# Attention of a graph network block: softmax weights normalised ahead of their transposes, and the product with v on four column tiles

## The reference

```python
x = _layernorm(x + _L0_gnn_ref(x, adj, ...))   # two layers: u = h W h' masked by adj, exp, divide, @ h_lin, norm, relu
x = _layernorm(x + _L1_gnn_ref(x, adj, adj, Wq, Wk, Wv, bv, Wo, bo))

# _L1_gnn_ref, 12 heads of 32 features
q, k, v = x @ Wq.T, x @ Wk.T, x @ Wv.T + bv
scores = einsum('bqhd,bkhd->bhqk', q, k) * scale + (adj + adj)[:, None]
row_nonzero = any(scores != 0, axis=-1, keepdims=True)
p = nan_to_num(softmax(where(row_nonzero, scores, -inf)))
out = einsum('bhqk,bkhd->bqhd', p, v).reshape(b, n, h)
return out @ Wo.T + bo
```

## Time and profile before

| | |
|---|---|
| median of three runs | 2868.6 us (2867.44 to 2870.93) |
| profiled execution | 2869.89 us, its span 2868.0 us |
| PE busy | 2794.6 us, 97% |
| PEld busy | 1790.0 us, 62% |
| DVE busy | 2406.5 us, 84% |
| ACT busy | 1770.5 us, 62% |
| POOL busy | 1657.6 us, 58% |
| DMA | 112.21 MB, 39 GB/s in the mean |

### The profile page before, as it was taken

The page is one execution under the profiler, slowest core; times in us unless marked ns, Lnnn a source line. Parts: engine busy times, 40 slices in busy tenths (PEclk is TensorE's granted clock), DMA queues, the critical chain, the costliest instruction groups (busy, mean ns, idle before and its releaser), DMA issues.

```text
span 2868.0 us, 69803 instructions
## 1 busy us (share of the span) xinstructions
PE 2794.6 (97%) x24768; PEld 1790.0 (62%) x24768; DVE 2406.5 (84%) x8042; ACT 1770.5 (62%) x4107; POOL 1657.6 (58%) x2097
## 2 busy tenths in 40 slices
PE   7999999999999999999999999999999999999996
PEld 4566666666665666666666656666666666566664
DVE  5788888888888888888888888888888888888886
ACT  4556666556665556665566655566655666555664
POOL 2556565556565565655565655656555656555554
PEclk9999999999999999999999999999999999999998
DMA  4001011111011010111010110101110101101000
GB/s 151 30 32 45 21 46 40 41 36 34 32 43 43 32 45 21 45 40 44 33 35 31 43 43 31 45 21 45 40 45 32 41 25 43 43 32 45 21 27 21
DMA packets 55976, 112.21 MB, mean 39 GB/s; under 512 B 4944, under 2 KB 37712, under 8 KB 55632
## 3 DMA queue, kind: packets, MB, share of 16 engines
q1 hardware_dynamic: 55632, 107.76, 11.0%
HBM read 82.58 MB, written 25.17 MB: 38 GB/s over the span
## 4 chain that ended last, share of the span: by engine, by line
PE 86%; DVE 10%; ACT 2%; issue 1%; POOL 0%; DMA 0%; DVEq 0%; SPq 0%; POOLq 0%; ACTq 0%
PE psum L1250 62%; PE psum L1260 11%; PE psum L1311 9%; PE psum L1404 3%; PE psum L1378 2%; DVE z L1016 2%; DVE nT_lo L813 2%; DVE pT_lo L811 1%; DVE rs L876 1%; DVE qk_lo L813 1%; ACT qk_hi L536 1%; ACT pT_hi L536 1%; DVE st L915 1%; DVE o L888 1%; DVE y L907 1%
## 5 line engine op out<-in xcount | busy, mean ns | idle before, releaser
L596 ACT ACTIVATE w<-s,nmax 128x128 f32<-128x128 f32 x1536 | 479.4, 403 | 1.9 <-DVE nmax L846 1.9
L1250 PE MATMUL psum<-hT_hi,w_hi 128*128 128x512 f16 x1152 | 439.1, 381 | 13.3 <-POOL hT_lo L379 11.9
L1250 PE MATMUL psum<-hT_lo,w_hi 128*128 128x512 f16 x1152 | 438.7, 381 | 0.0
L1250 PE MATMUL psum<-hT_hi,w_lo 128*128 128x512 f16 x1152 | 438.4, 381 | 0.0
L536 ACT ACTIVATE nT_hi<-psum 128x512 f16<-128x512 f32 x384 | 230.1, 599 | 271.0 <-PE psum L1250 270.9
L463 POOL TENSOR_TENSOR fold<-fold 128x384 f32<-128x384 f32 (+4 forms) x640 | 342.8, 536 | 50.1
L846 DVE CUSTOM_DVE_ANT_0 s<-psum,adj 128x128 f32<-128x128 f32 x1536 | 341.0, 284 | 30.8 <-PE psum L1378 30.0
L463 POOL TENSOR_TENSOR fold<-s 128x768 f32<-128x768 f32 x128 | 242.3, 1893 | 193.5 <-DVE nmax L846 193.5
L387 POOL TENSOR_TENSOR hl_lo<-hl_raw,hl_hi 128x384 fp32r<-128x384 f32 x256 | 245.3, 963 | 147.5 <-ACT hl_hi L536 143.6
L811 DVE TENSOR_TENSOR pT_lo<-psum,pT_hi 128x512 f16<-128x512 f32 x384 | 253.2, 683 | 37.7 <-ACT pT_hi L536 37.5
L536 ACT ACTIVATE pT_hi<-psum 128x512 f16<-128x512 f32 x384 | 222.0, 598 | 85.3 <-PE psum L1260 85.1
(11 more groups left out here) (133 smaller groups left out, 7948.5 us busy)
## 6 DMA issues: line engine op xcount, KB each, us to landing
xTin<-xT SPq DMA_DIRECT2D x32, 768.0 KB, 4.7
xres<-x SPq DMA_DIRECT2D x32, 768.0 KB, 4.6
out<-y SPq DMA_DIRECT2D x128, 192.0 KB, 1.9
adjn<-adj SPq DMA_DIRECT2D x32, 256.0 KB, 4.9
adjT_sb<-adjT SPq DMA_DIRECT2D x32, 256.0 KB, 5.0
adj<-adj SPq DMA_DIRECT2D x32, 256.0 KB, 2.8
x<-weights SPq DMA_DIRECT2D x4, 576.0 KB, 5.4
s<-weights SPq DMA_DIRECT2D x3, 576.0 KB, 6.4
```

Source lines behind the costliest of these rows:

```text
L596: last = nc.scalar.activation(w[:, m], s[b % 2][:, m], ACT.Exp, bias=nmax[b % 2][:, m:m + 1], scale=-1.0)
L1250: last = mm(dst, a, b, start=(i == 0), stop=(i == total - 1))
```

## The change

`v` loses its column of ones, and the row sums come from ACT: the exponentials have an `accum_out` into `sums`. Once all 12 heads of a graph are done, DVE makes reciprocals (`rcp`) and `rs`, and POOL multiplies w by rs in three parts (`norm`), in place, before PE transposes it. w has two buffers. In `pv` the operands change places: 32 columns of v are stationary, 128 columns of pT move, and the four heads j of a step write to the four 32-partition quarters of one bank. The output so comes out transposed, and the split into oT_hi and oT_lo reads it straight from the bank of `pv`; the stage `to` on PE and the product `o` on DVE go. The folds on POOL stop at 16 columns and DVE does the rest in one `tensor_reduce`. `v_raw` has two buffers instead of four. The bank lists and the orders of PE, DVE, ACT and POOL are new; pt(3), norm(3) and rs(3) move to the next pass. The order on SP stays.

```diff
-        w = sb("w", [HEADS, TOK])
+        w = [sb(f"w{i}", [HEADS, TOK]) for i in range(2)]
@@ banks
-                "pt": pt_lo, "pv": o_ok, "to": to_lo, "po": y2_ok}
+                "pt": pt_lo, "pv": to_lo, "po": y2_ok}
...
-        TAIL = (("pv", 3), ("to", 3), ("po", 3), ("fin", 2), ("fin", 3), ("y2_power", 3), ("store", 3))
+        TAIL = (("rs", 3), ("norm", 3), ("pt", 9), ("pt", 10), ("pt", 11), ("pv", 3), ("po", 3), ("fin", 2), ("fin", 3), ("y2_power", 3), ("store", 3))
@@ POOL
-                for n, src_ok, done in ((TOK // 2, None, fold1), (TOK // 4, fold1, fold2), (TOK // 8, fold2, fold3),
-                                        (TOK // 16, fold3, fold4), (TOK // 32, fold4, fold5),
-                                        (TOK // 64, fold5, fold6)):
+                for n, src_ok, done in ((TOK // 2, None, fold1), (TOK // 4, fold1, fold2), (TOK // 8, fold2, fold3)):
...
-                nc.gpsimd.tensor_tensor(total[b % 2][:], fold[:, :, 0], fold[:, :, 1], ALU.add)\
-                    .then_inc(s_tot.sem, 1)
+            def norm(run, b, r):
+                p = run.of("norm", b)
+                if p is None:
+                    return
+                if r == 0:
+                    pool.wait_ge(rs_ok.sem, p.upto(rs_ok, b + 1))
+                part = slice(TILES * r, TILES * (r + 1))
+                nc.gpsimd.tensor_tensor(w[b % 2][:, part], w[b % 2][:, part],
+                                        rs[b % 2][:, part, None].to_broadcast([128, TILES, TOK]), ALU.mult)\
+                    .then_inc(pn_ok.sem, 1)
@@ ACT exps
-                if b > 0:
-                    act.wait_ge(pt_full.sem, p.upto(pt_full, KB * (b - 1) + chunk))
+                if b >= 2:
+                    act.wait_ge(pt_full.sem, p.upto(pt_full, KB * (b - 2) + chunk))
+                    act.wait_ge(rcp_ok.sem, p.upto(rcp_ok, b - 1))
...
-                    last = nc.scalar.activation(w[:, m], s[b % 2][:, m], ACT.Exp, bias=nmax[b % 2][:, m:m + 1],
-                                                scale=-1.0)
+                    last = nc.scalar.activation(w[b % 2][:, m], s[b % 2][:, m], ACT.Exp, bias=nmax[b % 2][:, m:m + 1],
+                                                scale=-1.0, accum_out=sums[b % 2][:, m:m + 1])
@@ DVE live_of, rs_of
+                dve.wait_ge(fold3.sem, p.upto(fold3, b + 1))
+                nc.vector.tensor_reduce(total[b % 2][:], fold[:, :, 0:TOK // 8], AX.X, ALU.add).then_inc(s_tot.sem, 1)
...
+                dve.wait_ge(p_ok.sem, p.upto(p_ok, (b + 1) * TILES))
+                nc.vector.reciprocal(rcp[b % 2][:], sums[b % 2][:]).then_inc(rcp_ok.sem, 1)
...
+                nc.vector.scalar_tensor_tensor(rs[b % 2][:], live[b % 2][:], 0.0, rcp[b % 2][:], ALU.is_gt, ALU.mult)\
+                    .then_inc(rs_ok.sem, 1)
@@ DVE v
+                if b >= 2:
+                    dve.wait_ge(vr_lo.sem, p.upto(vr_lo, b - 1))
@@ PE pt, pv
-                pe.wait_ge(p_ok.sem, p.upto(p_ok, TILES * b + r + 2))
-                turn("pt", n, [w[:, TILES * r + i] for i in range(TILES)], pt_full)
+                pe.wait_ge(pn_ok.sem, p.upto(pn_ok, n + 1))
+                turn("pt", n, [w[b % 2][:, TILES * r + i] for i in range(TILES)], pt_full)
...
-                for n in range(HEADS):
-                    h = TILES * (n % KB) + n // KB
-                    terms = split(pT_hi[b % 2][:, n], pT_lo[b % 2][:, n], v_hi[:, b, h], v_lo[:, b, h])
-                    for i, (a, m) in enumerate(terms):
-                        last = mm(dst[:, n * VCOL:(n + 1) * VCOL], a, m, start=(i == 0), stop=(i == 2))
+                for c in range(KB):
+                    for i in range(3):
+                        a, m = ((v_hi, pT_hi), (v_lo, pT_hi), (v_hi, pT_lo))[i]
+                        for j in range(TILES):
+                            d = slice(HEAD * j, HEAD * (j + 1))
+                            last = mm(dst[d, c * TOK:(c + 1) * TOK], a[:, b, c * 128 + HEAD * j:c * 128 + HEAD * (j + 1)],
+                                      m[b % 2][:, KB * j + c], start=(i == 0), stop=(i == 2))
```

More of the change, by code:

```diff
@@ L226, in await_apart, with await_bank @@
                 eng.wait_ge(sig.sem, value)
-            def await_bank(self, eng, stage, *parts):
-                last = {}
+            def await_bank(self, eng, stage, *parts, also=()):
+                last = {name: (self.group(READ[name]), i) for name, i in also}
                 for i in parts:
@@ L608, in round_e, with pt @@
                     copy(e_hi[:, 2 * h:2 * h + 2], e[:, 2 * h:2 * h + 2]).then_inc(e_hi_ok[l].sem, 1)
-            def pt(p, b, r):
-                if not p.l1:
+            def pt(run, b, r):
+                p = run.of("pt", KB * b + r)
+                if p is None:
                     return
@@ L756, in body @@
                 exps(p, 3, 0)
                 exps(p, 3, 1)
+                to(p, 1)
+                pt(p, 2, 0)
+                pt(p, 2, 1)
+                exp_u(p, 1, 0)
+                pt(p, 2, 2)
+                exp_u(p, 1, 1)
+                hl(p, 1, 2)
+                round_e(p, 1, 0)
+                xt(p, 2)
+                fin(p, 3)
+                hl(p, 1, 3)
+                round_e(p, 1, 1)
+                to(p, 2)
+                fin(p, 0)
+                ctx(p, 1, 0)
@@ L849, in scores, with pt @@
                 last.then_inc(s_ok.sem, 1)
-            def pt(p, b, r):
-                if p.l1:
+            def pt(run, b, r):
+                p = run.of("pt", KB * b + r)
+                if p is not None:
                     part = slice(TILES * r, TILES * (r + 1))
@@ L1159, in body @@
                 v(p, 1)
+                scores(p, 1, 0)
+                th(p, 1)
+                scores(p, 1, 1)
+                th(p, 2)
+                scores(p, 1, 2)
+                scores(p, 1, 3)
+                live_of(p, 0)
                 v(p, 2)
+                scores(p, 2, 0)
+                scores(p, 2, 1)
                 v(p, 3)
-                th(p, 1)
-                scores(p, 1, 0)
-                th(p, 2)
-                scores(p, 1, 1)
-                setup(p, 6)
@@ L1167, in body @@
-                scores(p, 1, 2)
-                pt(p, 0, 0)
-                setup(p, 7)
-                scores(p, 1, 3)
+                rs_of(p, 0)
+                scores(p, 2, 2)
+                nl(p, 1, 0)
+                scores(p, 2, 3)
+                hl(p, 1, 0)
+                live_of(p, 1)
+                hl(p, 1, 1)
+                scores(p, 3, 0)
+                pt(p, 0, 0)
+                scores(p, 3, 1)
+                nl(p, 1, 1)
+                fin(p, 3)
+                scores(p, 3, 2)
```

466 lines of the change are left out of this document (208 added, 258 removed).

## The result

The kernel after takes 2914.5 us (median of 4 runs, 2908.6 to 2917.3) against 2868.0 (4 runs, 2867.3 to 2870.9): a ratio of 1.0157, 95% interval 1.0139 to 1.0175. It is slower by 46.5 us, where 78 us less was forecast, and it lies above the range. The span of the profiled execution is 2914.0 us at a mean granted clock of 0.987 (before: 0.992).

A forecast was written before the change was run, and what follows sets the result against it. PE, busy 97% of the span, was taken as the bound. 2868.0 - 75.5 (pv and transposes) - 17 (wait for o) + 12 (new waits) + 2 (end) = 2789.5 us, given as 2790; range 2770 to 2880.

The forecast's parts named there:

- `pv` and `to`: On PE: pv takes 0.70 us instead of 0.91, o's transposes (0.38) go; 0.59 us a graph, 75.5 us less.
- B: In pv on PE: weight loads of column tiles queue, +0.54 us a graph, +69 us, 2859; chance 0.06.
- C: In pv on PE: column tiles run one after another, 2.2 us instead of 0.70, +192 us, 2980; chance 0.04.
- That a microsecond taken from PE comes off the time: On PE, busy 97% of the span: a saving there shortens the time if the other engines keep their hand-overs.
- In the queues themselves: On SP: its waits are for output rows and inputs it has long before; nothing put in the sum.
- The new waits: Hand-overs in a pass's second half: four within 0.5 us, jitter costs 0.4 us a pass, 12 us in all.
- POOL: Three normalising products a graph at 1.27 us; POOL 72% busy; its slowing of DVE, 5 us, left out of the sum.
- rival A: The chain through POOL is late, PE waits for w at the transposes; 2815 to 2865; chance 0.17.
- The exponentials' sums: On ACT: a sum output costs 0.08 us each, 48 a pass, 3.9 us; it fits in the second half.
- Rival D: On ACT: the sum output holds ACT up, 0.2 us a read, decisive from about 0.17; 2902; chance 0.14.
- DVE's reduction: On DVE: a new reduction of 128x12x16 per graph takes 0.33 us, 42 us in all, beside PE.
- The ends: Last pass: shorter pv to oT_lo but three POOL products ahead, net +2 us; the start practically unchanged.

The follow-up runs named there:

- e8: The kernel before with pv in column tiles, no transposes of o, its division left out, and the oT copies moved up on ACT and DVE: 2859.0 us.
- e12: e11 without the exponentials' sum output and with each normalising product on 8 of 128 columns: 2827.6 us.
- e1: The kernel after with the store of graph 2's row moved behind the next pass's loads on SP: 2887.2 us.
- e3: e1 with the load of xres also moved ahead of the store of block 3 on SP: 2881.3 us.
- e13: e3 with fin(3) moved up to after v(2) in ACT's order: 2852.3 us.
- e14: The kernel after with fin(3) alone moved up to after v(2) in ACT's order, SP's order as it is: 2881.6 us.
- e9: e3 with a third buffer for y2 and fin(3) moved up to after v(2) in ACT's order: 2852.2 us.
- e7: e3 with a third buffer for y2 and the normalising products on 8 of each 128 columns: 2839.4 us.
- e6: e3 with a third buffer for y2 and without the exponentials' sum output: 2863.3 us.
- e10: e9 with, in the last group alone, graph 3's factors and products ahead of graph 2's output statistics: 2852.6 us.
- e15: e10 with graph 3's last two sets of exponentials also moved up on ACT in the last group: 2854.9 us.
- e16: e11 with the second group's xTin load, in the first pass, issued ahead of the seventh weight's on SP: 2853.6 us.
- e17: e13 with the second group's xTin load, in the first pass, issued ahead of the seventh weight's on SP: 2855.0 us.
- e11: e10 with the roundings of the weights in the first pass put later again: 2863.3 us.

## Why the prediction was wrong, step by step

- **`pv` and `to`**: right. 0.71 us for 0.70, the transposes gone; rivals B and C are out. (B's price was a slip: 9 x 0.109 + 0.20 less 0.70 is 0.48 us a graph and 61 us, not 0.54 and 69.) The Trainium skill, TensorEngine Tiling (Array Packing), section Restrictions, has column tiling without the fast weight load. The rows show no price for it with 128x32 loads, 0.057 us a group of four as in the row tiles.
- **That a microsecond taken from PE comes off the time "as long as the other engines keep their hand-overs"**: the condition failed. e8 has the saving on PE and none of the added work, and gains 9 us. A busy share of 97% did not mean that PE alone set the pass: once PE's part is shorter, hand-overs through DVE, ACT and POOL are as long, and the earlier trace rows cannot show it, since a wait appears only then. e12 shows the other half: in the new order, with two places repaired and sums and products cut, 2.2 us a pass do come off.
- **"In the queues themselves: SP's waits are for output rows and inputs it has long before"**: the step that failed worst. It looked at when SP's inputs are ready and not at who now asks for what SP loads: `xt(0)` had moved up by 24 us while the load stayed where it was, `fin(3)` had moved down to where ACT's next steps were wanted, and nothing in the sum priced either. Price: 27 to 33 us for SP's order (e1, e3, e13 against e14), 29 to 33 for the place of `fin(3)` (e9, e13, e14).
- **The new waits, "0.4 us a pass"**: the walk covered PE against POOL and DVE in a pass's second half and found no gap there; that half is mostly not where it went wrong. The waits that came are at the boundary and in the first half, where I had counted room by busy time, and the one for `oT_lo` (21.7 us), late in the second half, is that of `fin(3)`.
- **POOL**: the product is 1.07 us instead of 1.27, so the term was over-sized; rival A (PE waiting at the transposes for w) shows almost only in the last groups, four of six waits and 15.3 of 16.2 us. What POOL does to DVE was seen, priced at 5 us and left at nothing "on an engine with 400 idle". The products cost 42 us (e7), most of it 1.2 us a pass, beside which DVE's slower scale_z is 4 x 0.262 = 1.05 us a pass by the rows and `var` 2 x 0.27. The operation that I had priced, `hT_lo`, became faster (756 ns in the mean, 917 before), though POOL is busy during 81% of its time in both kernels; why is open. The Trainium skill, GPSIMD Engine Reference, Specifications, says that the two engines share SBUF interfaces and contend when DVE has two SBUF inputs. scale_z is of that kind, and e7 agrees with it. The places of an engine's idle time matter, not their sum.
- **The exponentials' sums**: starts 0.385 us apart instead of 0.29, so 0.095 us each for 0.08 taken. The term was counted as hidden, and e6 gives it 18 us. Rival D needed 0.17 a read, and its marks are nearly absent: DVE waits 24.2 us for `pT_hi` (37.5 before) and 21.3 for `nT_hi` (11.7), PE at `u` 1.4 us for `nT_lo`. That its 2902 lies nearest to the measured time is luck.
- **DVE's reduction**: 0.34 for 0.33, right.
- **The ends**: +2 us was forecast (its own figures give 1.4), +11 at the last group and 8 at the first mark, 5 without its shift, came. e10, e15, e16 and e17 did not bring them back; their cause is open but for the products (in e7 the last group is 2.4 us shorter). In the last group the granted clock is lower too: from the last mark to the last matmul it is 0.75 in the mean over 68.3 us, half of them at the lower level, and was 0.86 over 57.6. In e12 it is 0.83 over 61.7. What of the 11 us is the clock and what the chain was not separated.

As a ledger over the mean pass, 31 of them: forecast 84.8; e12, the PE work in the repaired order, 85.18, 0.4 more or 12 us; with sums and products 86.24 (e13), 33 us more; with SP's order as it was 87.17 (e14), 29 us more; with `fin(3)` late 88.27, 34 us more. These four make 108 (31 x 3.48) of the 124.5 us between forecast and time; the first mark (8) and the last group (11, of which 2 were forecast) make the other 17.

A version that beats both: e13, the changed kernel with two places moved in SP's and ACT's orders, computes the whole reference in 2852.3 us, 0.58% under the kernel before and 2.1% under the kernel after. e12's 2827.6, which leaves out sums and most of the products, says that the normalisation ahead of the transposes costs at least 36 us here, against e11.

## What to carry to other kernels

When a static order is rewritten, list for each in-order queue what each entry waits for and who waits for what stands behind it, DMAs and stores too; a step that nobody needs, like an output row, belongs in a gap and not ahead of one that the next stage wants. An engine at 97% is one of the bounds and need not be the only one: before pricing a saving on it, look for the stretches in which another engine runs without a gap, before the change and in the new order, and expect to lose the saving there unless that stretch is shortened as well. Work that "fits into idle time" is to be put against that stretch and not against the engine's share of the span.

## What the runs showed of the hardware

- Four column tiles of 32 run abreast as four row tiles do: a group of four 128-column f16 matmuls every 0.057 us, with a different 128x32 load for each (kernel after).
- ScalarE's sum output is an instruction of its own, 0.19 us in its row; the exponentials' starts go from 0.29 to 0.385 us apart, 0.095 more. VectorE's, 0.08 us, starts together with the next operation.
- scale_z, a DVE operation of 128x384 with two large inputs in SBUF, takes 0.60 us alone and 0.87 or 1.39 beside GpSimd's broadcast products (e13); over all four of a pass the mean is 0.87. Cutting the products' columns to 8 of 128, with their count unchanged, brought 0.607 us back (e7). An operation on four elements took 0.80 us beside them, and `nT_lo`, with one input in PSUM, 0.68 with and without.
- A 192 KB store issued 1.3 us behind a 768 KB load landed after 4.1 us, where stores usually take 1.9 (kernel after).
